# Feed-forward layer norms of a fused eight-layer network: statistics over token rows instead of over channels

## The chip, the cores and the metric

One Trainium2 chip, one of its cores. The metric is device time in microseconds, the median of several executions. Engines: TensorE (PE, its weight loads PEld), VectorE (DVE), ScalarE (ACT), GpSimd (POOL), SyncE (SP), which here only issues transfers. PSUM has 8 banks of 128 partitions x 512 fp32; TensorE writes there, and GpSimd works in SBUF alone here.

## The reference

x and ctx are 16 batches x 128 tokens x 128 channels, fp32. In outline:

```
x = x + xattn0(layernorm(x), ctx)          # 16 heads
x = x + net0(layernorm(x))                 # 6 layers, 16 heads of 64, window 32
x = x + xattn1(layernorm(x), ctx)
x = x + net1(layernorm(x))                 # 2 layers, 8 heads of 64, window 64

def layer(x):                              # of net0 and net1
    x = x + local_attention(shift(x) @ Wqkv) @ Wo
    h = shift(x)                           # half of the channels from the token before
    xn = (h - mean(h)) / sqrt(var(h) + 1e-5) * g + b      # over the 128 channels
    a, gate = split(xn @ W1 + b1)          # 2 x 341
    return x + (a * gelu(gate)) @ W2 + b2
```

## The kernel before

The state z lies in SBUF as channels x tokens (128 partitions are the channels). Attention works batch by batch; the feed-forward part works on groups f of four batches, 128 x 512: 24 groups in the first network (f = 0 to 23), 8 in the second (24 to 31).

Everything is written out by hand: each engine has its own instruction list, in a software pipeline of steps s. Step s of the first network (`step_0`, s = 0 to 98) takes queries and keys of batch s, rotates and normalises them, turns batch s - 1, and does probabilities, values and output projection of batches s - 2 and s - 3. Each batch has two units i of eight heads. In the second network (`step_1`, s = 96 to 113) a step is a pair of batches. Between engines only semaphores order the work; an engine that waits holds all that stands behind it in its list.

The feed-forward work is laid into these steps: `ff_phase` gives for step s a place c and a group f. In the first network one group takes four steps (c = 0 to 3, called step 0 to step 3), in the second two. All its products go through PSUM bank 2, one after another. Within a step there are numbered slots. For a group, in the order of time:

- step 0, slot 0: TensorE `ff_mean` (a product with a matrix of 1/128, L835); VectorE `ff_centre` (L2238); ScalarE `ff_square` (L1621).
- step 0, slot 1: TensorE `ff_down` of the group before (three chunks, L877); VectorE `ff_close` (L2284).
- step 0, slot 2: TensorE `ff_var` (L841, four pairs of passes of two columns each, which give the variance of a token on its own partition); VectorE `ff_newton`, RSQ = 11 dependent operations on 128 x 4 values for 1/sqrt (L2248 to L2261), with scratch in bank 2.
- step 1, slot 0 (second network: step 0, slot 3): TensorE `ff_broadcast` (four transposes of a broadcast column, L849); VectorE `ff_normalise` (L2267); ScalarE `ff_affine` (L1628).
- then `ff_gate`, GELU, `ff_up` (L859, L868), VectorE copies and products (L2272, L2278).

The attention part has its own Newton iteration `newton(p)`, 11 operations on 128 x 32 values (L2182 to L2200, the last writes `rnorm`), also with scratch in bank 2; `row_max_all` (L2215) stands between them. TensorE may use bank 2 for step s only when it is done (`normal_free`). GpSimd then multiplies queries and keys by `rnorm` (`normal`, L1935, four per step), and TensorE turns them (`turn`, L731). GpSimd's list per step is: add (queries of unit 1, the step before; L1928), four `normal`, add, divide (L1942), two adds, divide. Its first `normal` is the queries of unit 0, which TensorE turns right after slot 0.

In the second network the order around slot 2 and 3 is, on VectorE: row maximum (L2207), `ff_newton`, residual (L2234), rotate of unit 1's queries (L2128, L2133), row sum (L2229), `ff_normalise`, rotate of unit 1's keys; on TensorE: `ff_var`, output projection (L823), queries of unit 1 (L710), probabilities (L798), `ff_broadcast`, keys and values of unit 1 (L710), turns (L731), `ff_gate`. On ScalarE `ff_square` stands behind the copies of the turned queries and keys (L1559, two).

Group 23 runs between the networks, among the steps of the second cross-attention (`between`); the last group is done in two halves by functions of its own.

## Time and profile before

| | us |
|---|---|
| median of 3 runs (2283.44 to 2286.98) | 2284.48 |
| span of the profiled execution | 2282.5 |
| TensorE busy | 2130.3 (93%) |
| VectorE busy | 1788.6 (78%) |
| ScalarE busy | 1686.7 (74%) |
| GpSimd busy | 1339.8 (59%) |

The profile gives the profiled execution's own time as its span, from the first to the last instruction; it stands 2.0 us below the median of the runs. A row of a timeline is a stretch of like instructions of one engine: where it starts, how long it lasts, how many they are, and in brackets the idle time in front and what ended it. An fp32 product is two passes (two MATMUL rows); passes overlap at their ends, so the distance from start to start tells what one occupies.

### The profile page before, as it was taken

Reading aid. Unit: us, or ns where it says so; the run is one execution under the profiler, and the core shown is the slowest. Engines: PE = TensorE matmul, PEld = TensorE weight load, DVE = VectorE, ACT = ScalarE, POOL = GpSimd, SP = SyncE. Lnnn points to the kernel's source line nnn. Section 1 sums busy time; section 2 is a strip of 40 time slices with the busy share of each in tenths; the row PEclk is TensorE's granted clock in tenths of the full one; section 3 lists DMA queues with packets and bytes.
Section 4 is the critical chain, followed back from the end, with each engine's and each line's share of the span. In section 5 each row is a group of like instructions: output and inputs, shape, how many; then the busy total and the mean of one; then the engine's idle time right before and its main releaser. Section 6 shows DMA issues by size and latency. Waiting matters only on the chain. (4 is left out here: it accounts for less than half of the span.)

```text
span 2282.5 us, 88445 instructions
## 1 busy us (share of the span) xinstructions
PE 2130.3 (93%) x33790; PEld 1460.0 (64%) x33790; DVE 1788.6 (78%) x5019; ACT 1686.7 (74%) x5850; POOL 1339.8 (59%) x1270
## 2 busy tenths in 40 slices
PE   7988999999999999999999999999999886899997
PEld 5656666666666666666666666666666664666664
DVE  4988887878788878887788787887887478787873
ACT  3757787788778878787787787877777544788884
POOL 1337666666667666666666666766665124766660
PEclk8999999999999999999999999999999998999999
DMA  4001221112211222112211122211221100000001
GB/s 113 4 3 37 71 60 45 41 46 67 52 43 45 62 52 53 43 45 64 55 48 40 43 69 58 50 39 44 54 55 40 45 10 10 13 13 16 13 9 28
DMA packets 144799, 96.93 MB, mean 42 GB/s; under 512 B 61976, under 2 KB 137408, under 8 KB 144384
## 3 DMA queue, kind: packets, MB, share of 16 engines
q1 hardware_dynamic: 143232, 91.02, 15.7%
q8 instruction: 274, 4.49, 0.8%
q14 instruction: 141, 1.16, 0.2%
q10 hardware_dynamic: 1152, 0.26, 0.1%
HBM read 23.11 MB, written 1.05 MB: 11 GB/s over the span
## 5 line engine op out<-in xcount | busy, mean ns | idle before, releaser
L1935 POOL TENSOR_TENSOR arena<-arena,rnorm 128x512 f32<-128x512 f32 x448 | 455.2, 1044 | 382.5 <-DVE rnorm L2200 381.3
L710 PE MATMUL bank<-wqkv,hs 128*128 128x512 f32 x1344 | 668.0, 617 | 7.8 <-issue 2.8
L1928 POOL TENSOR_TENSOR arena<-arena 128x512 f32<-128x512 f32 x448 | 566.8, 1273 | 96.1 <-DVE arena L2133 96.0
L1582 ACT ACTIVATE arena<-bank,amx 128x64 f32<-128x64 f32 x1536 | 457.6, 335 | 4.6 <-DVE amx L2215 4.3
L2128 DVE TENSOR_TENSOR arena<-bank,rot 128x512 f32<-128x512 f32 x448 | 306.7, 685 | 75.1 <-PE bank L710 70.2
L710 PEld LDWEIGHTS bank<-wqkv,hs 128*128 128x128 f32 x1344 | 231.4, 192 | 189.2 <-issue 168.0
L1582 ACT ACTIVATION_READ_ACCUMULATOR arena<-bank,amx 128x1 f32 x1536 | 351.8, 229 | 0.0
L1559 ACT ACTIVATE arena<-bank 128x512 f32<-128x512 f32 x426 | 249.8, 619 | 116.0 <-PE bank L731 114.7
L2133 DVE TENSOR_TENSOR arena<-bank,rot 128x256 f32<-128x256 f32 x896 | 333.2, 413 | 0.0
L731 PEld LDWEIGHTS bank<-ident,arena 128*128 128x128 f32 x1792 | 212.8, 142 | 177.4 <-issue 127.7
L1942 POOL TENSOR_TENSOR arena<-arena,ainv 128x512 f32<-128x512 f32 x192 | 200.2, 1043 | 193.3 <-DVE ainv L2223 193.3
L2154 DVE TENSOR_REDUCE ss<-arena 128x8 f32<-128x512 f32 x448 | 283.0, 668 | 23.9 <-ACT arena L1553 23.7
L1553 ACT ACTIVATE arena<-bank 128x512 f32<-128x512 f32 x448 | 266.0, 642 | 42.3 <-DVE arena L2133 41.0
L731 PE MATMUL bank<-ident,arena 128*128 128x128 f32 x1792 | 256.9, 276 | 33.7 <-ACT arena L1590 20.3
L1613 ACT ACTIVATE arena<-bank 128x256 f32<-128x256 f32 x340 | 111.9, 381 | 201.4 <-PE bank L790 200.6
L823 PEld LDWEIGHTS bank<-arena,wo 128*128 128x128 f32 x1792 | 220.8, 194 | 55.1 <-issue 44.0
L823 PE MATMUL bank<-arena,wo 128*128 128x128 f32 x1792 | 225.9, 278 | 3.1 <-ACT arena L1613 2.7
L790 PE MATMUL bank<-arena 64*64 64x32 f32 (+1 forms) x9216 | 186.5, 221 | 42.1 <-issue 40.5
L790 PEld LDWEIGHTS bank<-arena 64*64 64x64 f32 x9216 | 160.1, 134 | 64.2 <-issue 46.2
L767 PE MATMUL bank<-arena 64*32 64x64 f32 (+1 forms) x12288 | 169.4, 217 | 0.0
L2215 DVE TENSOR_REDUCE amx<-bank 128x4 f32<-128x256 f32 x384 | 143.4, 414 | 30.3 <-PE bank L767 27.9
L767 PEld LDWEIGHTS bank<-arena 64*32 64x32 f32 x12288 | 155.9, 105 | 0.3
(214 smaller groups left out, 3260.1 us busy)
## 6 DMA issues: line engine op xcount, KB each, us to landing
arena<-arena SPq DMA_DIRECT2D x768, 64.0 KB
wqkv<-in_L_ffn_Wqkv_dram SPq DMA_DIRECT2D x24, 256.0 KB
hs<-z SPq DMA_DIRECT2D x128, 32.0 KB, 1.8
hs<-z SPq DMA_DIRECT2D x128, 31.8 KB, 1.9
fx<-z SPq DMA_DIRECT2D x31, 128.0 KB, 2.2
fx<-z SPq DMA_DIRECT2D x31, 127.0 KB, 2.5
wqkv<-in_L_ffn_Wqkv_dram SPq DMA_DIRECT2D x24, 128.0 KB
w<-in_L_ffn_W_dram SPq DMA_DIRECT2D x6, 341.0 KB
```

Of the source, the lines that this page charges most:

```text
L710: nc.tensor.matmul(bank[o][:], src[:], wqkv[w][:, off:off + 512], start=True, stop=True).then_inc(AT[name] if part < 2 else AT[name][i], 1)
L731: mm = nc.tensor.transpose(bank4[o][:, j, :], rc[i][c][p % 2][:, j * P:(j + 1) * P], ident[:])
L767: mm = nc.tensor.matmul(bank[3 + g][q:q + 32, DH * j:DH * j + n], q_t[i][rows, P * j + q:P * j + q + 32], k_t[i][rows, P * j + key:P * j + ...
L790: mm = nc.tensor.matmul(bank4[7 - half][to:to + DH, j, q0:q1], src[g][rows, DH * h:DH * h + DH], pbt[i][0][rows, h * P + q0:h * P + q1], s ...
L823: mm = nc.tensor.matmul(bank4[7][:, 0, :], wo[w][:, i, j, :] if ni == 0 else wo[w][:, j // 2, j % 2, :], o_t[i][:, j * P:(j + 1) * P], sta ...
L1553: nc.scalar.activation(sq[i][c], bank[c][:], ACT.Square).then_inc(AT["sqk" if c else "sqq"], 1)
L1582: ins = nc.scalar.activation(pb[i][0][p % 2][:, h * DH:(h + 1) * DH], bank[3 + g][:, j * DH:(j + 1) * DH], ACT.Exp, bias=amx[p % 2][:, i, ...
L1928: nc.gpsimd.tensor_tensor(t, t, rs[i][c], ALU.add).then_inc(AT["ak" if c else "aq"][i], 1)
L1935: nc.gpsimd.tensor_tensor(t, t, rnorm[p % 2][:, i, HU * c:HU * c + HU].unsqueeze(2).to_broadcast([P, HU, DH]), ALU.mult).then_inc(AT["mk" ...
L2128: nc.vector.tensor_tensor(heads(rc[i][c][p % 2]), src, r[:, 2 * c, :].unsqueeze(1).to_broadcast([P, HU, DH]), ALU.mult)
L2133: ins = nc.vector.tensor_tensor(dst, src[:, :, (1 - a) * hd:(2 - a) * hd], r[:, 2 * c + 1, a * hd:(a + 1) * hd].unsqueeze(1).to_broadcast( ...
L2154: nc.vector.tensor_reduce(ss[:, i, HU * c:HU * c + HU], heads(sq[i][c]), AX.X, ALU.add).then_inc(AT["ssk" if c else "ssq"], 1)
```

## The change

The layer norm of a group is done on tiles turned to token rows, for groups 0 to 30. `fx` (channels x tokens) is turned by four transposes into bank 2 (`ff_tokens` on TensorE, in the place of `ff_mean`), ScalarE copies it to SBUF (in the place of the square), and VectorE takes mean and variance of each token with `bn_stats` and `bn_aggr` (`ff_stats`, at slot 2 in front of `ff_newton`). `ff_centre` and `ff_var` are gone. The normalisation is done in place on the token rows: in the first network by GpSimd in two operations at the end of its list of step 0, in the second by VectorE in four `tensor_scalar` at slot 3, where `ff_normalise` stood. Then TensorE turns the tile back (`ff_channels`, four transposes, in the place of `ff_broadcast`), and ScalarE's affine reads bank 2. In the first network `ff_normalise` leaves VectorE. The last group's halves keep their way; only the names of their semaphores and a count differ.

```diff
+        ftok = quads(fcen)
+        f_st = sb("f_st", [P, 4, 6])
+        f_mv = sb("f_mv", [P, 4, 2])
...
-                at(sp, FF["cen"], f)
+                at(sp, FF["in"], f)
...
-                def ff_mean(f, s):
+                def ff_tokens(f, s):
                     normal_free(s)
                     at(pe, FF["hid"], 3 * f)
                     pe.wait_ge(FF["x"], 32 * (f + 1))
-                    nc.tensor.matmul(bank[2][:], mean_w[:], fx_f, start=True, stop=True).then_inc(FF["mean"], 1)
-
-                def ff_var(f):
+                    for j in range(4):
+                        mm = nc.tensor.transpose(bank4[2][:, j, :], fx[:, j, :], ident[:])
+                    mm.then_inc(FF["in"], 1)
+
+                def ff_channels(f, s):
+                    normal_free(s)
                     at(pe, FF["z"], f)
-                    pe.wait_ge(FF["sq"], f + 1)
+                    pe.wait_ge(FF["xn"], 2 * f + 2)
                     for j in range(4):
-                        mm = nc.tensor.matmul(bank[2][:, 2 * j:2 * j + 2], fsq[:, j * P:(j + 1) * P], mean_w[:, 0:2],
-                                              start=True, stop=True)
-                    mm.then_inc(FF["var"], 1)
-
-                def ff_broadcast(f, s):
-                    normal_free(s)
-                    pe.wait_ge(FF["rstd"], RSQ * (f + 1))
-                    for j in range(4):
-                        mm = nc.tensor.transpose(bank4[2][:, j, :], fy[3][:, j:j + 1].to_broadcast([P, P]), ident[:])
+                        mm = nc.tensor.transpose(bank4[2][:, j, :], ftok[:, j, :], ident[:])
                     mm.then_inc(FF["bc"], 1)
...
                 def ff_down(f, s):
                     normal_free(s)
-                    at(pe, FF["cen"], min(f + 2, 4 * (ph["layer0"] + ph["depth"])))
+                    at(pe, FF["tok"], min(f + 2, 4 * (ph["layer0"] + ph["depth"])))
...
                     if c == 0 and f >= 0 and slot_ == 0:
-                        ff_mean(f, s)
+                        ff_tokens(f, s)
...
-                    if c == 0 and f >= 0 and slot_ == 2:
-                        ff_var(f)
                     if c == 1 and f >= 0 and slot_ == 0:
-                        ff_broadcast(f, s)
+                        ff_channels(f, s)
...
-                def ff_square(f):
-                    act.wait_ge(FF["cen"], f + 1)
-                    at(act, FF["var"], f)
-                    nc.scalar.activation(fsq, fcen, ACT.Square).then_inc(FF["sq"], 1)
+                def ff_tokens(f):
+                    act.wait_ge(FF["in"], f + 1)
+                    at(act, FF["bc"], f)
+                    nc.scalar.activation(fcen, bank[2][:], ACT.Copy).then_inc(FF["tok"], 1)
...
-                    act.wait_ge(FF["xn"], f + 1)
+                    act.wait_ge(FF["bc"], f + 1)
...
-                    nc.scalar.activation(fxn, fxn, ACT.Identity, scale=lnp[w][:, 0:1], bias=lnp[w][:, 1:2]
+                    nc.scalar.activation(fxn, bank[2][:], ACT.Identity, scale=lnp[w][:, 0:1], bias=lnp[w][:, 1:2]
...
+                def ff_normalise(f):
+
+                    pool.wait_ge(FF["rstd"], RSQ * (f + 1))
+                    nc.gpsimd.tensor_tensor(ftok, ftok, f_mv[:, :, 0].unsqueeze(2).to_broadcast([P, 4, P]), ALU.subtract
+                                            ).then_inc(FF["xn"], 1)
+                    pool.wait_ge(FF["xn"], 2 * f + 1)
+                    nc.gpsimd.tensor_tensor(ftok, ftok, fy[3][:].unsqueeze(2).to_broadcast([P, 4, P]), ALU.mult
+                                            ).then_inc(FF["xn"], 1)
...
                     if live(s - 2):
                         divide_all(1, s - 2)
+                    c, f, before = ff_phase(ph, s)
+                    if c == 0 and f >= 0:
+                        ff_normalise(f)
...
-                def ff_centre(f):
-                    dve.wait_ge(FF["mean"], f + 1)
-                    nc.vector.tensor_tensor(fcen, fx_f, bank[2][:], ALU.subtract).then_inc(FF["cen"], 1)
+                def ff_stats(f):
+                    dve.wait_ge(FF["tok"], f + 1)
+                    for j in range(4):
+                        ins = nc.vector.bn_stats(f_st[:, j, :], ftok[:, j, :])
+                    ins.then_inc(FF["st"], 1)
+                    dve.wait_ge(FF["st"], f + 1)
+                    for j in range(4):
+                        ins = nc.vector.bn_aggr(f_mv[:, j, :], f_st[:, j, :])
+                    ins.then_inc(FF["mv"], 1)
...
-                            dve.wait_ge(FF["var"], f + 1)
-                            var = bank[2][:, 0:8].rearrange("p (b a) -> p b a", a=2)[:, :, 0]
-                            ins = nc.vector.tensor_scalar(f_s, var, EPS, None, ALU.add)
+                            dve.wait_ge(FF["mv"], f + 1)
+                            ins = nc.vector.tensor_scalar(f_s, f_mv[:, :, 1], EPS, None, ALU.add)
...
                 def ff_normalise(f):
-                    dve.wait_ge(FF["bc"], f + 1)
-                    nc.vector.tensor_tensor(fxn, fcen, bank[2][:], ALU.mult).then_inc(FF["xn"], 1)
+                    dve.wait_ge(FF["rstd"], RSQ * (f + 1))
+                    for j in range(4):
+                        ins = nc.vector.tensor_scalar(ftok[:, j, :], ftok[:, j, :], f_mv[:, j, 0:1], fy[3][:, j:j + 1],
+                                                      ALU.subtract, ALU.mult)
+                    ins.then_inc(FF["xn"], 2)
...
                     if c == 0 and f >= 0 and slot_ == 2:
+                        ff_stats(f)
                         ff_newton(f)
-                    if c == 1 and f >= 0 and slot_ == 0:
-                        ff_normalise(f)
```

In the second network's lists `ff_mean` and `ff_broadcast` are replaced in their places as above (slots 0 and 3), `ff_var` and `ff_centre` go, and VectorE keeps `ff_normalise` at slot 3. For group 23 GpSimd's `ff_normalise` follows its step 1 of the cross-attention.

## Rows read from the trace of the kernel before

**Rows 1.** The page's first part: busy time of each engine.
```profile
span 2282.5 us, 88445 instructions
...
PE 2130.3 (93%) x33790; PEld 1460.0 (64%) x33790; DVE 1788.6 (78%) x5019; ACT 1686.7 (74%) x5850; POOL 1339.8 (59%) x1270
```
**Rows 2.** Waits of TensorE, 280 to 1760 us: total, times, longest.
```profile
PE bank L731 <- ACT arena L1590: 20.3, 22, 1.1
PE bank L731 <- POOL arena L1935: 3.7, 13, 0.5
```
**Rows 3.** Timeline of TensorE, step 0 to step 1: start, length, line, count.
```profile
1552.46 2.74 PE L877 MATMUL bank<-arena,w 128*128 128x512 f32 x6
...
1556.77 0.95 PE L841 MATMUL bank<-mean_w,arena 128*128 128x2 f32 x8
1557.58 1.07 PE L731 MATMUL bank<-ident,arena 128*128 128x128 f32 x8
...
1564.31 0.63 PE L731 MATMUL bank<-ident,arena 128*128 128x128 f32 x4 [0.26 <-POOL arena L1935]
```
**Rows 4.** Timeline of VectorE, the same stretch.
```profile
1556.02 1.23 DVE L2154 TENSOR_REDUCE ss<-arena 128x8 f32<-128x512 f32 x2
1557.76 0.17 DVE L2248 TENSOR_SCALAR bank<-bank 128x4 f32<-128x4 f32 x1 [0.52 <-PE bank L841]
...
1559.77 0.16 DVE L2261 SCALAR_TENSOR_TENSOR fy<-bank,fy 128x4 f32<-128x4 f32 x1
...
1562.78 0.19 DVE L2200 SCALAR_TENSOR_TENSOR rnorm<-bank,ny 128x32 f32<-128x32 f32 x1
```
**Rows 5.** Timeline of GpSimd, the same stretch.
```profile
1557.18 1.27 POOL L1928 TENSOR_TENSOR arena<-arena 128x512 f32<-128x512 f32 x1
1563.12 3.04 POOL L1935 TENSOR_TENSOR arena<-arena,rnorm 128x512 f32<-128x512 f32 x3 [4.67 <-DVE rnorm L2200]
```
**Rows 6.** Groups by line, whole trace: busy us, mean ns, idle before.
```profile
L2234 DVE TENSOR_TENSOR z<-bank,z 128x128 f32<-128x128 f32 x128 | 37.1, 290 | 29.8 <-PE bank L823 26.7
...
L2267 DVE TENSOR_TENSOR arena<-arena,bank 128x512 f32<-128x512 f32 x31 | 19.8, 640 | 0.6 <-PE bank L849 0.6
```
**Rows 7.** Timeline of TensorE, second network, first step of a group.
```profile
2112.90 1.02 PE L835 MATMUL bank<-fx,mean_w 128*128 128x512 f32 x2
2113.76 1.02 PE L710 MATMUL bank<-wqkv,hs 128*128 128x512 f32 x2
...
2115.49 2.74 PE L877 MATMUL bank<-arena,w 128*128 128x512 f32 x6
...
2124.33 0.60 PE L849 MATMUL bank<-ident,fy 128*128 128x128 f32 x4
2124.77 1.88 PE L710 MATMUL bank<-wqkv,hs 128*128 128x512 f32 x4
```
**Rows 8.** Timelines of ScalarE and VectorE in that step.
```profile
2115.26 1.08 ACT L1559 ACTIVATE arena<-bank 128x512 f32<-128x512 f32 x2
2116.23 0.63 ACT L1621 ACTIVATE arena<-arena 128x512 f32<-128x512 f32 x1
...
2121.22 0.68 DVE L2207 TENSOR_REDUCE amx<-bank 128x4 f32<-128x512 f32 x1
2121.82 0.16 DVE L2248 TENSOR_SCALAR bank<-bank 128x4 f32<-128x4 f32 x1
...
2125.35 0.17 DVE L2229 RECIPROCAL ainv<-asum 128x4 f32<-128x4 f32 x1
```
**Rows 9.** Timeline of TensorE between the networks, at group 23.
```profile
1821.57 0.62 PE L849 MATMUL bank<-ident,fy 128*128 128x128 f32 x4 [0.52 <-DVE fy L2261]
```
**Rows 10.** An idle stretch of TensorE; two windows (busy, granted clock 0.50, 1.00, DMA).
```profile
1136.52 0.82 PE L790 MATMUL bank<-arena 64*64 64x32 f32 x28 [1.94 <-issue]
...
1136.90:1140.30 3.40, 3.40 (x21) 1.79 (x13) 0.92 (x2) 2.93 (x18) 3.40 (x4) 0.50 0.17 44
617.00:622.00 5.00, 2.88 (x26) 1.88 (x27) 2.85 (x8) 2.49 (x12) 4.10 (x4) 1.00 0.30 78
```

More of the change, by code:

```diff
@@ L173, in build @@
         ln_rsqrt = sem("ln_rsqrt")
-        FF = {n: sem("ff_" + n) for n in "x mean cen sq var rstd bc xn aff up ge gelu hid y z outer".split()}
+        FF = {n: sem("ff_" + n) for n in "x in tok st mv rstd bc xn aff up ge gelu hid y z outer".split()}
         XP = {n: sem("xp_" + n) for n in "p act dve".split()}
@@ L933, in feed_forward_1 @@
                     if c == 0 and f >= 0 and slot_ == 0:
-                        ff_mean(f, s)
+                        ff_tokens(f, s)
                     if c == 0 and before >= 0 and slot_ == 1:
                         ff_down(before, s)
-                    if c == 0 and f >= 0 and slot_ == 2:
-                        ff_var(f)
                     if c == 0 and f >= 0 and slot_ == 3:
-                        ff_broadcast(f, s)
+                        ff_channels(f, s)
                     if c == 0 and f >= 0 and slot_ == 4:
@@ L1235, in half_mean @@
                 pe.wait_ge(FF["x"], 32 * (32 + h))
-                nc.tensor.matmul(bank[o][:, 0:256], mean_w[:], half(fx_f, h), start=True, stop=True).then_inc(FF["mean"], 1)
+                nc.tensor.matmul(bank[o][:, 0:256], mean_w[:], half(fx_f, h), start=True, stop=True).then_inc(FF["in"], 1)
             def half_var(h, o):
-                pe.wait_ge(FF["sq"], 32 + h)
+                pe.wait_ge(FF["st"], 32 + h)
                 for j in range(2):
@@ L1658, in step_0 @@
                     if c == 0 and f >= 0:
-                        ff_square(f)
+                        ff_tokens(f)
                     if c == 1 and f >= 0:
@@ L1697, in step_1 @@
                     if c == 0 and f >= 0:
-                        ff_square(f)
+                        ff_tokens(f)
                     if live(s):
@@ L1725, in step_1 @@
                         outputs(0, s - 2)
-                return (step_0, ff_square, ff_affine, ff_gelu) if ni == 0 else (step_1, outputs)
+                return (step_0, ff_tokens, ff_affine, ff_gelu) if ni == 0 else (step_1, outputs)
             def y_project(p, a):
@@ L1989, in step_1 @@
                         add(0, s, 0)
-                return step_0 if ni == 0 else step_1
-            t0, t1 = pool_phase(PHASES[0]), pool_phase(PHASES[1])
+                return step_0 if ni == 0 else step_1, ff_normalise
+            (t0, ff0_normalise), (t1, _) = pool_phase(PHASES[0]), pool_phase(PHASES[1])
             def y_difference(p):
@@ L2029, in _ @@
                 y_step(s)
+                if s == 1:
+                    ff0_normalise(23)
             t1(96)
@@ L2338, in feed_forward_1 @@
                     if c == 0 and f >= 0 and slot_ == 2:
+                        ff_stats(f)
                         ff_newton(f)
```

24 lines of the change are left out of this document (10 added, 14 removed).

## The prediction

> **What bounds the kernel now.** I read the page first: TensorE is busy 93% of the span of 2282.5 us, VectorE 78%, GpSimd 59% [rows 1]. That invites the reading "take work off TensorE and gain", so the second view is who TensorE waits for. In the 1,480 us of the first network it waits by name for two things only: for ScalarE's L1590 (20.3 us, 22 times) and for GpSimd's L1935 (3.7 us, 13 times) [rows 2]. The second one is to be noticed, because it sits where this change works. Four steps serve one feed-forward group f; call them step 0 to step 3. The third view is the timeline of one step 0 and the start of step 1, engine by engine. TensorE runs without a gap from the down projection (L877) over the variance matmuls (L841, started 1556.77) to the broadcast, and then waits 0.26 us for GpSimd before it turns the queries at 1564.31 [rows 3]. VectorE follows: after L877 it closes the residual and sums squares until 1557.25, waits 0.52 us for L841, runs the 11 small operations of the layer norm's Newton iteration from 1557.76 to 1559.93, and then those of the attention norm, whose last write (rnorm) ends at 1562.97 [rows 4]. GpSimd starts L1935 0.15 us later, and the first of the three in its row ends about 1.04 us after that; TensorE's turn starts 0.15 us behind it [rows 5]. So the end of step 0 is set by one chain: L877, VectorE's close and sums, L841, 11 operations, 11 more with the row maxima between them, one GpSimd product, the turn. It was last, by name, in 13 of the 23 such steps; in the others TensorE's own work was as long. The two run level, so both have to get shorter for a gain.
>
> In the second network a group takes two steps, and its first (the row of 2112 to 2127) shows TensorE with no idle at all [rows 7]: there every microsecond that TensorE is made to wait goes into the time.
>
> **TensorE's work.** ff_mean goes: two passes that occupy 0.86 us (from 2112.90 to the next start at 2113.76) [rows 7]. ff_var goes: 0.81 us (1556.77 to 1557.58) [rows 3]. The broadcast's four transposes (0.44 us, from 2124.33 to the next start) [rows 7] become ff_channels at the same cost, and ff_tokens costs four more. Net per group 0.86 + 0.81 - 0.44 = 1.23 us less, 0.42 of it before L877 and 0.81 behind it; 31 groups, 38 us if nothing else bound.
>
> **VectorE's new work.** The centring and in the first network the product (L2267, 0.64 us) [rows 6] go, but neither stands in the chain above. What enters it is ff_stats: four bn_stats of 128 elements and four bn_aggr of 6. No row shows either. A 128-element operation takes 0.29 us [rows 6]; two of 512 elements that take 0.67 each last 1.23 together [rows 4], so one starts some 0.1 before the one in front ends, and four of 128 are 3 x 0.20 + 0.28 = 0.88 us. Small operations last 0.17 us [rows 4]; without a wait between them I take 0.08 apart: 3 x 0.08 + 0.165 = 0.40. With two gaps of 0.035 us as between chained small ones, and 0.08 of overlap with the sums in front, the block is 0.88 + 0.40 + 0.07 - 0.08, about 1.26 us. Bounds: below, eight operations at 0.10 us, half the distance at which chained small ones follow one another, 0.8 us; above, bn_stats at double cost (0.35 apart) and bn_aggr 0.2 us each, 4 x 0.35 + 0.8 + 0.1, about 2.3 us. I take 1.26, being nearest in size to the rows it is drawn from.
>
> **First network, step 0 to 1 (23 groups).** L877 and all behind it comes 0.42 us earlier. ff_tokens on ScalarE is ready by then, since L823 in front of L877 already waits for the ScalarE work in front of ff_tokens. VectorE's sums end at 1557.25 - 0.42 = 1556.83 and Newton starts at 1558.09 instead of 1557.76: +0.33. rstd is ready at 1560.26. Now GpSimd: ff_normalise is queued behind the last divide, but in front of the next step's add (L1928) and L1935. Before, that add was done at 1558.45, long before anyone needed it [rows 5]. Now: start 1560.40; two broadcast products of 1.04 us each, as L1935 with the same 128x512 and a broadcast input (three in 3.04 us) [rows 5], with 0.08 between them: 1562.56; the add, 1.24 (1.27 less the overlap): 1563.79; L1935, 1.0: 1564.8; TensorE turns at 1564.95 instead of 1564.31. That is **+0.64 us per group, 14.7 us for 23**. (rnorm, at 1563.30, is no longer last.) TensorE, 1.23 us earlier, gets all of it back as idle time: some 1.2 us ahead of ff_channels, which waits for rnorm because the Newton iteration uses the same bank 2 as scratch, and 1.1 us ahead of the turn. The bound from below (block 0.8) is +0.2 us a group, from above (2.3) +1.7. Behind that turn everything hangs on TensorE again and is shifted as a whole; the wait for L1590, in step 2, is no cushion, as ScalarE's run up to it starts from TensorE's value products.
>
> A sentence on GpSimd's price, which the sum can do without. The rows show 1.04 us for such a product on GpSimd against 0.64 on VectorE [rows 5, 6], a ratio of 1.6; the Trainium skill (GPSIMD Engine Reference, 3.1 Elementwise) makes ordinary elementwise work the wrong job for GpSimd and gives 1.96 for a two-input add. By that rule, as an estimate, two products would take 2 x 1.96 x 0.64 = 2.5 instead of 2.1 us, and the 24 groups of the first network another 10 us; the rows of this kernel decide, but the rule's direction, against this change, is also theirs.
>
> **Second network (groups 24 to 30).** Two new waits. First, L877 now waits for ff_tokens on ScalarE, which stands behind both L1559. Before, it started at 2115.49 [rows 7]. ScalarE's L1559 pair ends at 2116.34, 0.1 us earlier now, ff_tokens takes the place of L1621 (0.60 of its 0.63 us, less the overlap) [rows 8], and L877 starts at 2116.76: +1.27. Second, ff_channels now stands where the broadcast stood (2124.33), ahead of the second unit's keys, values and turns, and waits for VectorE's ff_normalise, while the broadcast only needed rstd. Count along VectorE [rows 8]: the second L2207 ends at 2121.90 + 1.27 = 2123.17, the block takes it to 2124.43, from there the old distance from L2248 to the end of L2229 (2121.82 to 2125.52, 3.70 us: 11 operations, a residual, one rotate, a reciprocal) to 2128.13, then four tensor_scalar of 128 elements, 0.80: 2128.93. TensorE starts ff_channels at 2128.98 instead of 2124.33: **+4.65 us**, of which it stands idle 4.2 in one piece. Groups 25 to 29 pay it, 23.3 us. Group 24 has no down projection in front, so not the first wait of 1.27: +3.3. Group 30 stands in the tail, where hardly anything else is queued on VectorE between rstd and the product: its +0.5 is an estimate.
>
> **Group 23**, between the networks: TensorE's broadcast at 1821.57 waited for rstd already [rows 9]. Now a block that starts Newton about 0.7 later and two GpSimd products (2.3 with their waits) stand in front: +3.0, with nothing beside it.
>
> Sum of waits and work: 14.7 + 23.3 + 3.3 + 3.0 + 0.5 = 44.8 us. The DMAs are the same; the load of fx is released earlier, by the transposes instead of the centring. ScalarE's square becomes a copy of the same size, and its affine only changes its input.
>
> **The clock.** The granted TensorE clock falls to half after some idle stretches: after 1.94 us of waiting for nothing named, 1136.9 to 1140.3 were granted at 0.50, which is 1.2 of 2.4 GHz [rows 10]. From 617 to 622, where TensorE was busy only 2.88 of 5 us, the clock stayed full [rows 10]. So an idle stretch of two microseconds may or may not be followed by a fall; each costs 3.4 x 0.5 = 1.7 us where TensorE is the bound, and behind both new waits it is. The waits of 4.2 us are longer than any of these: I count five falls, 8.5 us. Those of the first network come as 1.2 and 1.1 us with transposes between; step 2 has waits of up to 1.1 us today [rows 2], so I count only four in 23, 6.8 us; the ends are none and 23.
>
> **The sum.** Span 2282.5 + 44.8 + 15.3 = 2342.6; the median of the runs is 2.0 us above the profiled span, so **2345 us**, +2.6%.
>
> **Rivals.**
> - TensorE is the bound and the chain gives way (the other side): 93% busy speaks for it; the turn's wait for L1935 in 13 of the steps speaks against. 31 x 1.23 = 38 us less, 2246. It decides from the point where the turn's input is ready 1.2 us before TensorE asks for them today, that is 1.9 us sooner than I work out. Chance 0.04.
> - It does nothing measurable (gains in the first network offset the second's waits): 2280 to 2289, 0.03.
> - No further clock falls: 2284.5 + 44.8 = 2329, 0.25. For it: 617 to 622, where the clock did not fall.
> - A fall after every new wait: 28 x 1.7 = 48 instead of 15, 2377, 0.10.
> - A cheap stats block (0.8): 29 x 0.46 = 13 less on top of no falls, 2316, 0.07.
> - A dear block (2.3): 29 x 1.04 = 30 more, 2375, 0.06.
> - My forecast: 0.45.
>
> **How the numbers follow.** The range 2312 to 2378 holds the forecast and the four cases beside it; what lies outside are the first two and mixtures beyond the ends. 0.2% is 4.6 us, about what a measurement of this kernel tells from no change: faster 0.04, same 0.03, slower 0.93.
>
> **What would show it.** Right: in step 1 the turn (L731) waits for L1935, now behind two GpSimd operations of the layer norm and an add; ff_channels is late in the second network by about 4 us with VectorE's last tensor_scalar as releaser; L877 waits for ScalarE there; the two-step period of 41.4 us grows to about 46; bn_stats start near 0.2 us apart; more stretches at half clock. Wrong: TensorE idle unchanged with a shorter span, or a block far from 1.26 us.

## The result, and the profile after

The changed kernel takes 2357.81 us (median of 4 runs, 2349.14 to 2360.61) against 2285.73 for the kernel before, measured beside it: 1.0311 times as long, 95% interval [1.0288, 1.0334]. The forecast was 2345 in 2312 to 2378. The profiled execution has a span of 2356.7 us, 74.2 more than before. All times in this document are of executions in the chip's usual state: one of early_first_only's four (2413 us) and one of the kernel before (5202) were in a slower one and are left out. Lines have moved by a few: L875 is now the down projection, L734 the turn, L847 `ff_channels`, L839 `ff_tokens`, L2208 the attention norm's iteration with `rnorm`, L1929 GpSimd's `normal`, L1922 its add, L1942 and L1945 its two new products.

The page's first part, to be held against [rows 1]:

```profile
span 2356.7 us, 88305 instructions
PE 2120.1 (90%) x33604; PEld 1449.7 (62%) x33604; DVE 1806.6 (77%) x5233; ACT 1691.0 (72%) x5850; POOL 1389.2 (59%) x1318
```

TensorE has 10 us less work and the kernel is 74 longer, so all of the loss is waiting (and half clock, during which the busy time counts double). Where it arises is read by lining up the two executions at the same step: each step of the attention part ends with the write of `rnorm`. By step 95, the end of the first network's cycle, the changed kernel is 18.6 us behind; between the networks it loses 5.3 (one stretch of 145.4 us became 150.7); in the second network 45.3; in the tail, with group 30, 5.0. In the second network the first step of group 24 grew from 19.7 to 26.9 us and that of groups 25 to 29 by 7.0 to 8.7 (twice from 20.9 to 28.3, by 7.4), and the second step not at all.

The first network's 18.6 is the number of one execution. Four of the kernels below have the same first network (first_only, act_first, row_sum_after, pe_later), and theirs stand 11.9 to 17.8 us behind the kernel before at step 95. The changed kernel is 8.2 us behind at step 11 already, with two groups begun, the four others 0.6 to 4.9.

**First network.** The waits of TensorE from 280 to 1780 us (total, times, longest):

```profile
PE bank L793 <- issue: 43.8, 36, 1.9
PE bank L734 <- ACT arena L1584: 20.4, 21, 1.1
PE bank L734 <- POOL arena L1929: 17.3, 21, 0.9
PE bank L847 <- DVE rnorm L2208: 13.9, 16, 0.9
```

Against [rows 2], the turn's wait for GpSimd has gone from 3.7 to 17.3 us, and there is a new wait, of `ff_channels` for the end of the attention norm. The wait for ScalarE is what it was. Then one step 0 and the start of step 1, the places of [rows 3 to 5]. TensorE, VectorE, GpSimd (start, length, line, count, idle before):

```profile
1571.11 2.74 PE L875 MATMUL bank<-arena,w 128*128 128x512 f32 x6
...
1580.89 0.60 PE L779 MATMUL bank<-ident,arena 128*128 128x128 f32 x4
1582.38 0.66 PE L847 MATMUL bank<-ident,arena 128*128 128x128 f32 x4 [0.89 <-DVE rnorm L2208]
1583.89 0.63 PE L734 MATMUL bank<-ident,arena 128*128 128x128 f32 x4 [0.85 <-POOL arena L1929]
```
```profile
1575.81 0.86 DVE L2247 BATCH_NORM_STATS2 f_st<-arena 128x6 f32<-128x128 f32 x4
1576.70 0.38 DVE L2251 BATCH_NORM_AGGREGATE f_mv<-f_st 128x2 f32<-128x6 f32 x4
1577.12 0.17 DVE L2261 TENSOR_SCALAR bank<-f_mv 128x4 f32<-128x4 f32 x1
...
1582.14 0.19 DVE L2208 SCALAR_TENSOR_TENSOR rnorm<-bank,ny 128x32 f32<-128x32 f32 x1
```
```profile
1579.36 1.04 POOL L1942 TENSOR_TENSOR arena<-arena,f_mv 128x512 f32<-128x512 f32 x1 [3.49 <-DVE fy L2274]
1580.48 1.04 POOL L1945 TENSOR_TENSOR arena<-arena,fy 128x512 f32<-128x512 f32 x1
1581.48 1.26 POOL L1922 TENSOR_TENSOR arena<-arena 128x512 f32<-128x512 f32 x1
1582.70 2.04 POOL L1929 TENSOR_TENSOR arena<-arena,rnorm 128x512 f32<-128x512 f32 x2
```

From the down projection to the start of Newton it is now 6.01 us (before 5.30 [rows 3, 4]): the statistics are longer by 0.71 than the wait for the variance they replace. From there to the end of `rnorm` it is 5.21 in both. Then GpSimd: `rnorm` ends at 1582.33, and the first product starts 0.37 behind it instead of 0.15, because the row of three operations in front runs until 1582.74. The turn is 12.78 us behind the down projection instead of 11.85. The two waits of TensorE, 0.89 and 0.85, are about the 1.2 us of work it was freed of and the 0.44 by which a step's turn is now later.

**Second network.** TensorE, VectorE, GpSimd and ScalarE in the first step of a group, the places of [rows 7, 8]:

```profile
2159.46 0.60 PE L839 MATMUL bank<-ident,fx 128*128 128x128 f32 x4
...
2163.30 2.81 PE L875 MATMUL bank<-arena,w 128*128 128x512 f32 x6 [1.51 <-issue]
...
2176.57 0.78 PE L847 MATMUL bank<-ident,arena 128*128 128x128 f32 x4 [4.44 <-DVE arena L2281]
2177.15 3.46 PE L713 MATMUL bank<-wqkv,hs 128*128 128x512 f32 x4
2180.45 1.04 PE L734 MATMUL bank<-ident,arena 128*128 128x128 f32 x8
```
```profile
2169.70 0.86 DVE L2247 BATCH_NORM_STATS2 f_st<-arena 128x6 f32<-128x128 f32 x4
...
2174.55 0.16 DVE L2237 RECIPROCAL ainv<-asum 128x4 f32<-128x4 f32 x1
2174.63 1.80 DVE L2281 TENSOR_SCALAR arena<-arena,f_mv,fy 128x128 f32<-128x128 f32 x4
```
```profile
2174.79 1.05 POOL L1952 TENSOR_TENSOR arena<-arena,ainv 128x512 f32<-128x512 f32 x1 [5.80 <-DVE ainv L2237]
```
```profile
2162.52 0.69 ACT L1615 ACTIVATE arena<-bank 128x512 f32<-128x512 f32 x1
```

From the first use of bank 2 to the fourth it was 11.43 us (2112.90 to 2124.33 [rows 7]); it is 17.11, so 5.68 more. Of that 1.25 lies in front of the down projection (2.59 became 3.84). The profile puts that wait down to nothing by name, but ScalarE's copy of the token tile (L1615) ran from 2162.52 to 2163.21, and L875 follows 0.09 later. The rest is the statistics (1.31 us from the start of the first `bn_stats` to Newton), the residual and the rotate behind Newton, for which the broadcast did not have to wait, and the normalisation, 1.80 us instead of the 0.80 forecast. Behind it the four projections last 3.30 us to the next start instead of 1.72: half clock. Windows of three stretches (length, PE busy, PEld, DVE, ACT, POOL, granted clock, DMA share, GB/s):

```profile
280.00:1780.00 1500.00, 1401.42 (x26117) 966.25 (x26100) 1205.60 (x3591) 1172.74 (x4288) 1017.75 (x955) 0.99 0.20 50
2030.00:2290.00 260.00, 224.94 (x1877) 142.98 (x1879) 185.59 (x545) 177.95 (x542) 138.98 (x128) 0.95 0.04 11
2176.90:2180.30 3.40, 3.40 (x7) 1.48 (x6) 1.20 (x3) 0.78 (x1) 0.00 (x0) 0.50 0.02 5
```

The clock fell behind `ff_channels` in every group from 24 to 29, for 3.4 or 6.8 us each, and four times more in the tail. In the first network, from 280 to 1780 us, it fell four times (before, in the same part, five). The longest TensorE wait there is 0.9 us for a new reason, and 4.4 in the second network.

And the new operations by line (busy us, mean ns of one, idle before):

```profile
L2247 DVE BATCH_NORM_STATS2 f_st<-arena 128x6 f32<-128x128 f32 x124 | 26.6, 277 | 0.0
L2281 DVE TENSOR_SCALAR arena<-arena,f_mv,fy 128x128 f32<-128x128 f32 x28 | 11.9, 486 | 0.0
L2251 DVE BATCH_NORM_AGGREGATE f_mv<-f_st 128x2 f32<-128x6 f32 x124 | 11.7, 157 | 1.1
```

### The profile page after: what moved, and what is told of

Read it like the earlier page. It is cut to its first block and busy times, and to the rows that moved or that the text cites. A ratio compares the mean times of both kernels' runs of the same rounds, so it can differ in the third digit from the quotient of the medians.

```text
span 2356.7 us, 88305 instructions
## 1 busy us (share of the span) xinstructions
PE 2120.1 (90%) x33604; PEld 1449.7 (62%) x33604; DVE 1806.6 (77%) x5233; ACT 1691.0 (72%) x5850; POOL 1389.2 (59%) x1318
## 5 line engine op out<-in xcount | busy, mean ns | idle before, releaser
L713 PE MATMUL bank<-wqkv,hs 128*128 128x512 f32 x1344 | 676.1, 623 | 7.5 <-ACT arena L1547 2.5
L1922 POOL TENSOR_TENSOR arena<-arena 128x512 f32<-128x512 f32 x448 | 566.6, 1272 | 117.4 <-DVE arena L2141 117.2
L1929 POOL TENSOR_TENSOR arena<-arena,rnorm 128x512 f32<-128x512 f32 x448 | 455.4, 1045 | 280.8 <-DVE rnorm L2208 279.4
L1576 ACT ACTIVATION_READ_ACCUMULATOR arena<-bank,amx 128x1 f32 x1536 | 358.8, 234 | 0.0
L734 PEld LDWEIGHTS bank<-ident,arena 128*128 128x128 f32 x1792 | 213.9, 142 | 196.9 <-issue 140.9
L1553 ACT ACTIVATE arena<-bank 128x512 f32<-128x512 f32 x426 | 251.3, 625 | 100.4 <-PE bank L734 99.9
L1547 ACT ACTIVATE arena<-bank 128x512 f32<-128x512 f32 x448 | 268.1, 649 | 51.3 <-DVE arena L2141 48.1
L734 PE MATMUL bank<-ident,arena 128*128 128x128 f32 x1792 | 258.8, 277 | 48.9 <-POOL arena L1929 20.6
L826 PEld LDWEIGHTS bank<-arena,wo 128*128 128x128 f32 x1792 | 219.5, 193 | 58.3 <-issue 45.3
L1596 ACT ACTIVATE arena<-bank 128x512 f32<-128x512 f32 x224 | 141.9, 634 | 33.3 <-PE bank L713 33.0
```

The lines of the kernel that those rows point to most:

```text
L713: nc.tensor.matmul(bank[o][:], src[:], wqkv[w][:, off:off + 512], start=True, stop=True).then_inc(AT[name] if part < 2 else AT[name][i], 1)
L734: mm = nc.tensor.transpose(bank4[o][:, j, :], rc[i][c][p % 2][:, j * P:(j + 1) * P], ident[:])
L826: mm = nc.tensor.matmul(bank4[7][:, 0, :], wo[w][:, i, j, :] if ni == 0 else wo[w][:, j // 2, j % 2, :], o_t[i][:, j * P:(j + 1) * P], sta ...
L1547: nc.scalar.activation(sq[i][c], bank[c][:], ACT.Square).then_inc(AT["sqk" if c else "sqq"], 1)
L1553: nc.scalar.activation((k_t if c else q_t)[i], bank[5 + c][:], ACT.Copy).then_inc(AT["kte" if c else "qte"][i], 1)
L1576: ins = nc.scalar.activation(pb[i][0][p % 2][:, h * DH:(h + 1) * DH], bank[3 + g][:, j * DH:(j + 1) * DH], ACT.Exp, bias=amx[p % 2][:, i, ...
```

## The experiments

Twelve kernels, each timed against the kernel before on the same chip. Diffs are against the changed kernel.

| | us | ratio to before, 95% interval |
|---|---|---|
| first_only | 2300.85 | 1.0098 [1.0061, 1.0135] |
| second_only | 2330.45 | 1.0220 [1.0184, 1.0256] |
| early_first | 2296.98 | 1.0071 [1.0052, 1.0090] |
| early_second | 2356.01 | 1.0333 [1.0302, 1.0365] |
| early_first_only | 2242.78 | 0.9843 [0.9819, 0.9867] |
| row_sum_after | 2347.23 | 1.0286 [1.0263, 1.0309] |
| act_first | 2350.79 | 1.0315 [1.0278, 1.0352] |
| tuned_gate4 | 2255.33 | 0.9894 [0.9876, 0.9913] |
| stats_ahead | 2317.76 | 1.0152 [1.0127, 1.0176] |
| stats_twice | 2398.72 | 1.0498 [1.0455, 1.0541] |
| pe_later | 2334.04 | 1.0224 [1.0201, 1.0246] |
| tuned_gate5 | 2263.49 | 0.9912 [0.9881, 0.9942] |

**Each network alone.** The old functions stand beside the new ones, and a group takes one or the other:

```diff
+        NEW0, NEW1 = 0, 24            # second_only: 24, 31
+        def new(f):
+            return NEW0 <= f < NEW1
...
-                        ff_tokens(f, s)
+                        (ff_tokens if new(f) else ff_mean)(f, s)
-                        ff_channels(f, s)
+                        (ff_channels if new(f) else ff_broadcast)(f, s)
```

> The change in groups 0 to 23 alone; groups 24 to 30 keep the layer norm of before. Theory (both networks pay, each by its own chain): what the traces show up to the start of the second network's groups, +18.6 in the first network and +5.3 between the networks, so 2286 + 24 = 2310, and in a clean step 0 and 1 the end of the attention norm's Newton iteration comes 0.2 and 0.15 later than before. Rival (the first network loses nothing by the change, its +18.6 are chance stalls and clock falls, as it has 1.23 less TensorE work a group): 2265 to 2292.

> The change in groups 24 to 30 alone. Theory: +50 (seven first steps of a group at about +7.2 each, 5.8 of it waits and 1.6 a clock fall behind them), so 2336, with the two-step period at 48.8 instead of 41.4. Rival (part of the second network's loss comes from what the first leaves behind, buffers or the clock): clearly less than +50, under 2320.

Measured: +17.7 us by the medians for the first network alone, where 24 were expected (22 by the ratio, 14 to 31 from its ends, on 2283.1), and +47.3 for the second alone, where 50 were (50 by the ratio, 42 to 58). Both networks pay; the rival of a free first network (2265 to 2292) is out. The sum, 65 by the medians and 72 by the ratios, agrees with the 72 of the whole change within these intervals. In second_only the long steps have the lengths of the changed kernel (28.28, 29.57, 28.28, 27.95), so the second network's loss owes nothing to the first.

**The statistics and Newton off the chain, first network.** VectorE waits over 2 us for the down projection anyway. `early_first` does both there, `stats_ahead` only the statistics.

```diff
+                    if c == 0 and f >= 0 and slot_ == 1:
+                        ff_stats(f)
+                        ff_newton(f)          # early_first only
                     if c == 0 and before >= 0 and slot_ == 1:
                         ff_close(before)
-                    if c == 0 and f >= 0 and slot_ == 2:
-                        ff_stats(f)
-                        ff_newton(f)          # stays in stats_ahead
...
+        f_w = sb("f_w", [P, 12])              # early_first: scratch in SBUF
```

> The changed kernel, but in the first network VectorE's statistics and Newton iteration of the feed-forward norm stand ahead of the close of the group before, in time in which VectorE waits for the down projection, with the Newton iteration's scratch in SBUF instead of bank 2. Theory (the first network is level between this chain and TensorE): the chain of step 0 is over 2 us shorter, so TensorE's own work binds, which is 1.23 less a group than before: 0.37 + 1.2 less for each of 23 groups, 2358 - 36 = 2322. Rival (GpSimd's two products hold the next step's products back wherever the chain ends, or another engine is last): 2345 to 2358.

> The changed kernel; in the first network only the statistics (four bn_stats, four bn_aggr) stand ahead of the close of the group before, the Newton iteration stays behind the sums with its scratch in bank 2. Theory (first network: the chain down projection, close, sums, statistics, 11 operations, 11 more, GpSimd, turn): Newton starts 1.2 earlier, GpSimd's first product still follows two products of the layer norm and an add, so it starts 0.37 behind the end of the attention norm's iteration as now, and the turn 1.2 earlier: 23 groups, 2358 - 28 = 2330, with the wait ahead of ff_channels gone and a short one ahead of the turn. Rival (the first network's loss is GpSimd's queue alone): no more than 5 us off, 2350 to 2358.

Measured: early_first is 61 us under the changed kernel where 36 were expected, stats_ahead 40 where 28 were. The steps 0 of the first network in which TensorE has no stall (`rnorm` to `rnorm`) show the mechanism: 18.68 us before, 18.90 changed, 17.58 in stats_ahead, 16.60 in early_first. So stats_ahead gives the 1.3 it should (1.2 expected). The waits of TensorE from 280 to 1740 us in stats_ahead:

```profile
PE bank L734 <- POOL arena L1929: 9.7, 16, 0.7
```

The wait for `rnorm` is gone, and GpSimd's queue remains, 9.7 us of 17.3. In early_first, 280 to 1700 us, both are gone, and the ScalarE wait (in the kernel before it was that for L1590) and stalls without a name are nearly all that is left:

```profile
PE bank L794 <- issue: 34.9, 34, 1.9
PE bank L735 <- ACT arena L1585: 18.9, 20, 1.1
```

The four steps of a group take 66.4 us on average (before 68.1, changed 68.6): 1.7 less than before, of which 1.23 are TensorE's work and 0.4 the wait of the turn for GpSimd that the kernel before had (0.26 named in [rows 3], and 0.16 to restart). At 2.2 us a group, the 21 groups from step 11 to step 95 make 46 of the 61 us. Nearly 9 lie ahead of step 11, where the changed kernel's execution was late by itself: the four others with its first network are there 3.3 to 7.6 us earlier. Nearly 6 lie between the networks, where TensorE's wait for group 23's normalisation went from 4.4 to 2.0 us. So a few of the 61 us are chance, and stats_ahead too has 7.5 of its 40 ahead of step 11.

**A probe in the chain.** The four `bn_stats` are done twice.

```diff
+                    for j in range(4):
+                        nc.vector.bn_stats(f_xt[:, j, :], ftok[:, j, :])
```

> The changed kernel with the four bn_stats done twice, the first time into a buffer that nobody reads: a probe of 0.8 to 0.9 us put into the chain. Theory (the chain sets the end in both networks): all of it comes out, 30 groups at 0.85, 2358 + 26 = 2384. Rival (TensorE or something else binds in the first network, and its loss is chance stalls): only the second network's part, 2358 + 6 = 2364.

Measured: +41 over the changed kernel, more than the full price of the probe. It costs 0.78 us (1611.83 to 1612.61 between the two starts), and a step 0 without a stall is 0.77 longer (19.67): all of it comes out, as it must where the chain sets the end. Nearly all of the 41 arise up to step 95 (40.5), and the probe's share of them is 18. The rest is clock and stalls: TensorE's wait ahead of `ff_channels` reached 2.0 us, and from 280 to 1800 us the clock fell 17 times (in the changed kernel four times up to 1780); 13 more falls at 1.7 us would be 22, an estimate. From 280 to 1700 us it is 16 falls here and 3 to 9 in the five executions with waits of up to 0.9 us. But early_second, below, has such short waits and 15 falls, so the length of the wait alone does not tell how often the clock falls.

**Second network, one wait at a time.** `act_first` puts ScalarE's copy of the tokens ahead of the two copies of turned tiles; `row_sum_after` puts the reciprocal that releases GpSimd's divide behind the four `tensor_scalar`; `pe_later` puts `ff_channels` behind the second unit's keys, values and turns.

```diff
# row_sum_after, VectorE
-                    if live(s - 1):
-                        row_sum(0, s - 1, 0)
                     feed_forward_1(s, 3)
+                    if live(s - 1):
+                        row_sum(0, s - 1, 0)
# pe_later, TensorE
-                    if c == 0 and f >= 0 and slot_ == 3:
-                        ff_channels(f, s)
                     if c == 0 and f >= 0 and slot_ == 4:
+                        ff_channels(f, s)
                         ff_gate(f, 0, s)
```

> The changed kernel; in the second network ScalarE's copy of the token tile stands ahead of the copies of the turned queries and keys. Theory: the down projection no longer waits 1.3 us for ScalarE, and as everything up to ff_channels hangs on it the two-step period goes from 48.8 to 47.5 in groups 25 to 30, 2358 - 7 = 2350. Rival (the copies that are moved back by 0.6 us hold the scores back, or the wait only moves to ff_channels): 2356 to 2360.

> The changed kernel; in the second network VectorE's reciprocal of the first row sum, which releases GpSimd's divide, stands behind the four tensor_scalar instead of ahead of them, so that GpSimd is idle while they run. Theory (one of the four waits for GpSimd's divide to end, which the trace shows as 1.06 us against 0.33 of the others): the second takes 0.33, the four together 1.1 instead of 1.8 us, ff_channels comes 0.7 earlier (0.5 if the moved reciprocal's 0.17 counts in full), 6 groups, 2358 - 4 = 2354. Rival (a tensor_scalar with two column scalars takes 0.49 on its own): their length stays, 2358.

> The changed kernel; in the second network ff_channels stands on TensorE behind the second unit's keys, values and turns, directly ahead of ff_gate; nothing is moved on VectorE or ScalarE. Theory (TensorE's place in the queue is the loss: it stands 4.4 us idle with ready work behind it): 3.0 us of that work go ahead of the wait, the clock stays up, the gate waits about 0.9 for the affine: 7.4 less 3.0, less 1.6, plus 0.9 a group, 2358 - 24 = 2334. Rival (the ready work behind it feeds on engines that are themselves late, as ScalarE's affine stands ahead of the value and turn copies): 2350 or more.

Measured: act_first: the two-step period goes from 48.83 to 47.81, 1.0 of the 1.3 expected; 0.5 of the wait stays, as the copy still stands behind a square. Its ratio can't be told from the changed kernel's, the period can. row_sum_after is at 2347, where 2354 were expected; its ratio's interval, too, overlaps the changed kernel's. Its period is 47.99, 0.84 less, and VectorE's timeline with the line's group over the whole trace shows why:

```profile
2163.99 1.10 DVE L2281 TENSOR_SCALAR arena<-arena,f_mv,fy 128x128 f32<-128x128 f32 x4
2165.00 0.17 DVE L2237 RECIPROCAL ainv<-asum 128x4 f32<-128x4 f32 x1
```
```profile
L2281 DVE TENSOR_SCALAR arena<-arena,f_mv,fy 128x128 f32<-128x128 f32 x28 | 7.7, 340 | 0.0
```

340 ns instead of 486 for the same instruction: nothing was changed but when GpSimd works. The 486 were a mean of three at 0.33 and one at 1.06, which ended 0.08 behind GpSimd's divide every time. In group 30, where no GpSimd product runs beside them, the changed kernel's own four take 0.34 each. The rival, that two column scalars make it slow, is out.

pe_later came out at the 2334 that was written down. TensorE's timeline, to be held against the second network's above:

```profile
2161.52 1.04 PE L734 MATMUL bank<-ident,arena 128*128 128x128 f32 x8
2163.72 0.63 PE L847 MATMUL bank<-ident,arena 128*128 128x128 f32 x4 [1.16 <-DVE arena L2280]
2165.22 1.13 PE L857 MATMUL bank<-arena,w 128*128 128x512 f32 x2 [0.87 <-ACT arena L1621]
```

The wait of 4.44 is 1.16, a new one for the affine is 0.87, and the clock fell twice in the second network instead of in every group.

**The statistics, Newton and normalisation early in the second network.**

```diff
+                    if c == 0 and f >= 0 and slot_ == 1:
+                        ff_stats(f)
+                        ff_newton(f)
+                        ff_normalise(f)
                     if c == 0 and before >= 0 and slot_ == 1:
                         ff_close(before)
```

The calls at slots 2 and 3 go with it. ScalarE's copy stands first as in act_first, and Newton's scratch is in SBUF, in both networks.

> The changed kernel, but in the second network ScalarE's copy of the token tile stands ahead of the copies of the turned queries and keys, and VectorE's statistics, Newton iteration and normalisation stand ahead of the close of the group before; Newton's scratch is in SBUF in both networks. Theory (7.4 a group are these two waits and the clock fall that the longer one brings): both waits and the falls go, but VectorE's close comes some 3 us later than its input, of which TensorE has slack for a part: 2358 - 45 = 2313 if the close has slack, 2335 if all of the 3 us comes back. Rival (the waits are not the cause, the slower tensor_scalar and the block load VectorE as a whole): 2350 or more.

Measured: 2356, a miss of 20 to 40 us; the "rival" number came out, and not for its reason. VectorE and then GpSimd in that kernel, with TensorE behind them:

```profile
2173.74 0.17 DVE L2262 TENSOR_SCALAR f_w<-f_mv 128x4 f32<-128x4 f32 x1
2173.95 0.89 DVE L2266 TENSOR_SCALAR fy<-f_w 128x4 int32<-128x4 int32 x1
2174.87 0.96 DVE L2270 TENSOR_TENSOR f_w<-fy,f_w 128x4 f32<-128x4 f32 x1
2175.87 0.96 DVE L2272 SCALAR_TENSOR_TENSOR f_w<-f_w,fy 128x4 f32<-128x4 f32 x1
2176.86 1.19 DVE L2275 SCALAR_TENSOR_TENSOR fy<-f_w,fy 128x4 f32<-128x4 f32 x1
2178.09 0.16 DVE L2270 TENSOR_TENSOR f_w<-fy,f_w 128x4 f32<-128x4 f32 x1
```
```profile
2173.76 1.05 POOL L1953 TENSOR_TENSOR arena<-arena,ainv 128x512 f32<-128x512 f32 x1
2174.77 1.04 POOL L1930 TENSOR_TENSOR arena<-arena,rnorm 128x512 f32<-128x512 f32 x1
2175.77 1.04 POOL L1953 TENSOR_TENSOR arena<-arena,ainv 128x512 f32<-128x512 f32 x1
2176.77 1.26 POOL L1923 TENSOR_TENSOR arena<-arena 128x512 f32<-128x512 f32 x1
```
```profile
2183.81 2.08 PE L827 MATMUL bank<-arena,wo 128*128 128x128 f32 x8 [5.80 <-DVE z L2243]
```

Four operations on 128 x 4 values take 0.89 to 1.19 us. Each ends 0.02 to 0.03 us behind a GpSimd product (2174.84 behind 2174.81, 2175.83 behind 2175.81, 2176.83 behind 2176.81, 2178.05 behind 2178.03), and where GpSimd is idle it takes 0.16. With the scratch in bank 2 such operations are not held: in the kernel before, L2248 and its next three start 0.2 apart from 2121.82 on [rows 8], while a GpSimd product runs from 2121.82 to 2122.86, and in the changed kernel's step 0 the attention iteration runs undelayed under L1942, L1945 and the add. What Newton gained by its place it lost by its memory: 11 operations took 6.2 us instead of 2.2, the close came that late, and TensorE's wait, 5.80, only changed its name: from the end of step 96 to that of step 111 it is 348.1 us, and 348.0 in the changed kernel. No run has this order without the hold, so its share of the wait, 4.0 of the 5.8 us, is an estimate from the lengths of the operations. (Another 11 us are lost in its first network, where the clock fell 15 times from 280 to 1700 us; the steps 0 without a stall are as long as in the changed kernel, 18.8 against 18.9, and why the clock fell is open.) In early_first the same scratch cost hardly anything, as GpSimd was idle nearly every time.

The trace of the kernel before has this hold already, in the Newton iteration of another layer norm, whose scratch is in SBUF (VectorE, then GpSimd):

```profile
1959.57 1.18 DVE L281 SCALAR_TENSOR_TENSOR lt_a<-lt_y 128x4 f32<-128x4 f32 x1
1960.79 0.16 DVE L283 TENSOR_TENSOR lt_b<-lt_a,lt_s 128x4 f32<-128x4 f32 x1
```
```profile
1959.46 1.27 POOL L1928 TENSOR_TENSOR arena<-arena 128x512 f32<-128x512 f32 x1
```

The operation that started under the GpSimd add took 1.18 us and ended 0.02 behind it, and the next took 0.16. So it could have been read there before anything was forecast.

**Put together.** `early_first_only` is first_only with early_first. `tuned_gate4` has the new norm in both networks: early_first's order in the first; in the second act_first, row_sum_after, pe_later, the statistics ahead of the close, and Newton where it was with its scratch in bank 2. `tuned_gate5` moves the first `ff_gate` behind a unit's value products.

> First network as in early_first (statistics and Newton ahead of the close), second network with the layer norm of before. Theory: early_first is at 2297 of which the second network's groups cost 47 (second_only), so 2250, 1.5% below the kernel before; this is the change's gain without its loss. Rival (the two networks' parts don't add, the gain of early_first was in what followed group 23): 2265 to 2285.

> Both networks with the new layer norm. First network as early_first. In the second: ScalarE's copy first (act_first), the statistics ahead of the close of the group before, Newton where it was with its scratch in bank 2, the reciprocal behind the four tensor_scalar (row_sum_after), and on TensorE ff_channels behind the second unit's keys, values and turns, directly ahead of ff_gate. Theory (the 7.4 us a group are 1.3 ScalarE, 1.25 statistics, 3.2 that the normalisation ends later than the old broadcast could start, 1.6 clock): the first two go, the third is covered by the 3.0 us by which ff_channels is later, the clock stays up; the gate waits some 0.9 for the affine and TensorE has 1.2 less work, so the second network costs what it did before: 2250 to 2256. Rival (VectorE is then too late for the gate's copy, or the clock falls all the same): 2275 or more.

> As tuned_gate4 (2255), but in the second network ff_gate's first chunk stands behind the value products of unit 0 on TensorE, so that these cover the wait for the affine. Theory (of the 1.3 us by which a two-step period of tuned_gate4, 42.7, is longer than that of before, 0.9 are this wait): 2255 - 6 = 2249, level with the version that keeps the old layer norm in the second network (2246). Rival (the gate's copy on VectorE is then late, and the attention norm's iteration behind it): 2255 or more.

Measured: 2242.8, 1.6% under the kernel before and the fastest of all; 2250 were expected. tuned_gate4 is 2255.3, at the upper end of the 2250 to 2256 expected: the second network's two-step period is 42.7 (before 41.4, changed 48.8), at full clock throughout:

```profile
1990.00:2200.00 210.00, 196.37 (x1738) 126.82 (x1735) 166.23 (x505) 164.59 (x508) 127.15 (x118) 1.00 0.05 13
```

tuned_gate5, at 2263.5, missed its 2249: the wait for the affine was gone, but the value products, now first, ran into ScalarE's copy, which stands behind that affine (TensorE's waits, 1980 to 2260 us), and the period was 43.6:

```profile
PE bank L813 <- ACT arena L1598: 8.2, 6, 1.4
```

## Why the prediction was right

The direction, the time (2345 against 2357.8, so 60 of the 72 us of loss) and the mechanism held. In the second network the normalisation was priced too low; in the first the chain was priced at nearly twice what it cost, and stalls that nobody had forecast hid that. Term by term against the profiled span (forecast 2342.6, measured 2356.7):

| | forecast | measured |
|---|---|---|
| first network, waits and clock | 14.7 + 6.8 | 18.6 |
| between the networks (group 23) | 3.0 | 5.3 |
| group 24 | 3.3 | 7.2 |
| groups 25 to 29, waits and clock | 23.3 + 8.5 | 38.8 |
| rest of the second network's steps | 0 | -0.7 |
| tail, group 30 | 0.5 | 5.0 |

- **The statistics block, 1.26 us**: 1.23 from the end of the sums to Newton in the first network (1.31 from its own start, 1575.81 to 1577.12), 1.22 from the end of the row maximum in the second. The spacing of 0.20 and the 0.08 between small ones were right. The cheap and the dear block are out.
- **First network, turn 0.64 later a group**: Newton started 0.71 - 0.49 = 0.22 later (forecast 0.33), as the work freed ahead of the down projection was 0.49, not 0.42; GpSimd's chain added 0.22 (forecast 0.31). The turn is 0.44 later, and 0.37 of it reach the end of step 1: 8 us for 22 groups, not 14.7. The mechanism is shown by three runs (stats_ahead, early_first, stats_twice) that move the end by the length of what they move.
- **Its clock, 6.8 us**, four falls: from 280 to 1700 us the clock fell four times, as before. In the other kernels with this same first network it fell 9 (first_only), 9 (act_first), 3 (row_sum_after) and 6 times (pe_later), so one execution tells little, and two more than before is the mean. Beside it came stalls of TensorE without a releaser, 43.8 us in 36 pieces against 33.8 in 36 before. In the other kernels, from 280 to 1700 us, they are 39 to 43 where the turn waits for GpSimd behind the layer norm, and 33 to 37 where it does not, so they go with the late turn; what they are stays open. That the first network's 18.6 came near the 21.5 forecast is luck: the chain gives 8 of it, and the rest came with stalls and a late start that the prediction did not have.
- **Second network, L877 + 1.27**: 1.25, on ScalarE as said.
- **Four tensor_scalar, 0.80 us: the term that was mis-sized.** They took 1.80, for two reasons (row_sum_after). Alone they start 0.26 apart, not 0.20 (1.10 in all); and one of them is held for 0.73 while GpSimd divides, which the prediction hadn't looked for. `ff_channels` is then 5.68 later instead of 4.65: 1.0 too little in six groups.
- **The clock there, 1.7 a fall, five falls**: it fell in all six groups, 24 too. A fall cost 1.6 (3.30 instead of 1.72), and in groups 26 and 29, where the half clock lasted 6.8 us, the step grew by another 1.3 and 0.8. The period of two steps therefore became 48.5 to 50.4 us instead of the "about 46" given as a sign, which held the waits alone.
- **Groups 24, 23 and 30** were sized by hand: 24 has the same fall and normalisation as the rest, 3.9 more than forecast. At group 23 TensorE waited 4.42 us for GpSimd's second product, 3.9 more than the 0.52 of [rows 9], where 3.0 were forecast. In the tail TensorE waited 2.66 us for the normalisation in one piece and the clock fell again; that hardly anything else is queued on VectorE was no cover.
- **The rivals**: "TensorE bounds" (2246, 0.04) was false for this order. early_first_only comes near its number (2243) by another sum, 24 groups at 1.7 us instead of 31 at 1.23: the rival needed the chain 1.9 us shorter, and there the statistics and Newton, 3.5 us, are off it. The rule on elementwise work for GpSimd (Trainium skill, "GPSIMD Engine Reference", section 3.1 Elementwise) pointed the right way, but not in size: its two products took 1.04 us each as the rows of before said, and the first network's loss goes when they are only started earlier (early_first), on GpSimd still.

Here the trace bears out a rule of the Trainium skill that the prediction passed over. "SBUF — State Buffer", section "SBUF: two separate sides", says that a VectorE operation with two SBUF inputs, or in a mode that reads one through both ports, and a GpSimd operation lock each other out of a shared port for a whole instruction. Operations of both kinds were held here: `tensor_scalar` on SBUF took 1.06 instead of 0.33 us, two-input operations 0.96 instead of 0.16, and small operations with an input in PSUM were not held. `bn_stats` and `bn_aggr`, which read one SBUF tensor, took 0.84 and 0.38 for four while GpSimd's add ran (2172.53 to 2173.80 in early_second), as they do alone.

## What to carry to other kernels

A change that frees the busiest engine pays only where that engine also ends last: follow the chain through the step, and put new statistics into time in which their engine waits (the norm that lost 3.1% in its first order gained 1.1% in another, tuned_gate4, and 1.6% in the first network alone). An instruction that feeds an in-order queue is priced at what stands behind it: the same late tile cost 7.4 us a group in one place of TensorE's list, and 4.4 at the least where it stood 3 us of work further on and the clock stayed up (pe_later, two-step period 45.8). Before moving scratch or elementwise work into SBUF, look at when GpSimd runs.

## What the runs showed of the hardware

- VectorE operations with two inputs in SBUF, and `tensor_scalar` from SBUF to SBUF, waited for a running GpSimd product or add to end: 0.16 us became 0.89 to 1.19, and 0.33 became 1.06. With an operand in PSUM the same small operations stayed 0.2 apart, and `bn_stats` and `bn_aggr` were not held.
- Four `bn_stats` of 128 elements take 0.86 us and start 0.20 apart, four `bn_aggr` 0.38; `tensor_scalar` of 128 x 128 in SBUF 0.34, 0.26 apart.
- The clock fell to half right behind a TensorE wait of 4.4 us in all six groups, for 3.4 or 6.8 us; behind 1.16 us, with 0.87 a little later, in two of six.
